# The attention product of an adaLN block: tiles 10 to 15 in pairs, with seven products of half blocks

## The reference

```python
h = _layernorm(x, axis=-1) * (1 + ca) + sa
x = x + ga * _L0_attn_ref(h, mask, weight, bias)      # h @ (masked weight).T + bias, 1024 x 1024
h = _layernorm(x, axis=-1) * (1 + cb) + sb
x = x + gb * _L0_ffn_ref(h, gate_w, gate_s, up_w, up_s, down_w, down_s)   # silu(gate) * up, then down; 2752 wide
```

## Time and profile before

| | us |
|---|---|
| median of 3 runs | 1109.13 (1108.66 to 1110.12) |
| profiled execution | 1108.23 |
| its span, first to last instruction | 1106.2 |
| PE busy in the span | 1080.2 (98%) |
| DVE, ACT, POOL busy | 738.5, 427.8, 378.7 |
| attention products of all 16 tiles | 227.1 us busy as shown |

### The profile page before, as it was taken

The page is one execution under the profiler, slowest core; times in us unless marked ns, Lnnn a source line. Parts: engine busy times, 40 slices in busy tenths (PEclk is TensorE's granted clock), DMA queues, the critical chain, the costliest instruction groups (busy, mean ns, idle before and its releaser), DMA issues. The chain is left out here.

```text
span 1106.2 us, 13336 instructions
## 1 busy us (share of the span) xinstructions
PE 1080.2 (98%) x4753; PEld 501.8 (45%) x4753; DVE 738.5 (67%) x939; ACT 427.8 (39%) x783; POOL 378.7 (34%) x348
## 2 busy tenths in 40 slices
PE   5999999999999999999999999999999999999998
PEld 3444444545544444444444444444444444444444
DVE  4456578776687998889797888879545434334434
ACT  2322156555564554546555555555532000000000
POOL 2116346547643442325455555655200000000000
PEclk9999999999999999999999999999999999999999
DMA  9994313234453555445766666675289666566430
GB/s 343 387 388 118 89 64 95 78 94 162 148 200 129 166 175 164 133 125 163 205 204 177 180 200 180 184 204 178 77 350 335 244 248 241 220 241 239 191 127 38
DMA packets 132049, 206.94 MB, mean 187 GB/s; under 512 B 20624, under 2 KB 99216, under 8 KB 129552
## 3 DMA queue, kind: packets, MB, share of 16 engines
q1 hardware_dynamic: 126688, 184.08, 50.9%
q0 software_dynamic: 5296, 22.02, 5.6%
HBM read 137.39 MB, written 68.68 MB: 186 GB/s over the span
## 5 line engine op out<-in xcount | busy, mean ns | idle before, releaser
L1435 PE MATMUL pA<-work 128*128 128x512 f16 x1680 | 377.1, 379 | 4.4 <-ACT work L1099 2.6
L1435 PEld LDWEIGHTS pA<-work 128*128 128x128 f16 x1680 | 163.5, 98 | 205.1 <-ACT work L1099 6.5
L1238 PE MATMUL pA<-work 128*128 128x512 f32 x512 | 227.1, 595 | 2.5 <-DVE work L1694 0.9
L1435 PE MATMUL pB<-work 128*128 128x512 f16 x752 | 175.9, 379 | 1.4 <-DVE work L1855 1.4
L1238 PEld LDWEIGHTS pA<-work 128*128 128x128 f32 x512 | 94.3, 190 | 113.4 <-issue 110.4
L1877 DVE SCALAR_TENSOR_TENSOR work<-work 128x512 f16<-128x512 f16 x144 | 123.2, 878 | 19.1 <-ACT work L1119 18.8
L1502 PE MATMUL pA<-work 128*128 128x512 f16 x600 | 134.4, 379 | 0.0
L1099 ACT ACTIVATE work<-pA 128x512 f32<-128x512 f32 x126 | 74.6, 592 | 113.3 <-PE pA L1435 108.0
L1435 PEld LDWEIGHTS pB<-work 128*128 128x128 f16 x752 | 73.5, 98 | 90.1 <-DVE work L1855 2.1
L948 ACT ACTIVATE work<-pB,small 128x128 f32<-128x128 f32 x240 | 86.5, 476 | 69.5 <-PE pB L1211 58.1
L1502 PE MATMUL pB<-work 128*128 128x512 f16 x480 | 107.5, 379 | 0.5 <-DMA work<-h_left_scratch 0.5
(11 more groups left out here) (178 smaller groups left out, 1060.5 us busy)
## 6 DMA issues: line engine op xcount, KB each, us to landing
work<-h_scratch SPq DMA_DIRECT2D x8, 4480.0 KB, 13.7
h_scratch<-work SPq DMA_DIRECT2D x60, 512.0 KB, 3.3
work<-in_L_wmod SPq DMA_DIRECT2D x10, 2048.0 KB, 16.1
work<-in_L_ffn_gate_w SPq DMA_DIRECT2D x84, 128.0 KB, 3.3
work<-in_L_ffn_up_w SPq DMA_DIRECT2D x84, 128.0 KB, 3.0
work<-down_scratch SPq DMA_DIRECT2D x7, 1280.0 KB, 11.5
work<-in_L_ffn_down_w SPq DMA_DIRECT2D x68, 128.0 KB, 2.8
work<-in_L_attn_data SPq DMA_DIRECT2D x16, 512.0 KB, 4.3
```

What stands on the lines that cost most here:

```text
L1238: last = pe.matmul(pA[:, 2 * par(t) + h, :], hT1[par(t)][:, c, :], wT[:, c, h * H:(h + 1) * H], start=(c == 0), stop=(c == KT - 1))
L1435: last = pe.matmul(ps, w[:, m, c], bc[b][:, mv_, s, c], start=begin, stop=(i == n - 1 and c == KT // 2 - 1 and s == 1), skip_group_check=True)
```

## The change

Tiles 0 to 9 stay as they are. Tiles 10 to 15 are taken in three pairs (a, b). For a pair, the product of the two tiles (2 x 128 rows) by the weight (1024 x 1024) is seen as a 2 x 2 by 2 x 2 block product: a_11, a_12 are the two halves of the inner dimension of tile a, a_21, a_22 those of tile b, and w_11 to w_22 are quarters of the weight. Seven products of half blocks, with sums and differences of the a and w blocks, take the place of eight. In detail:

- POOL makes the weight combinations t_1, t_2, t_4 at tiles 3, 4 and 5 (`weight_combos`, two additions of 128 x 1024 each) and one more in place in the first pair; for each pair it makes four combinations of the turned inputs in place in `hT1` (128 x 512 each).
- PE runs the products 1, 2, 5, 6, 3, 4, 7 of four matmuls each, with four banks that change roles from pair to pair. One bank holds a running sum.
- ACT copies the running sum to `x1` three times a pair (four copies of 128 x 512), and turns tiles out in halves.
- DVE adds the other banks to these copies (five additions a pair), then multiplies by `ga` in SBUF.
- The weight combinations lie where rows 6 and 7 had their place (`bc0[3]`), so rows 6 and 7 now pass through `stage` and DRAM too, and are loaded back after the sixth product of the last pair; group 0 of the gate and up products waits for that load.
- The orders of all engines from tile 10 on are new.

The core of the diff:

```diff
-    bc_d = nc.dram_tensor("combos_scratch", (2, P, HE), F16).ap()
+    bc_d = nc.dram_tensor("combos_scratch", (3, P, HE), F16).ap()
...
+        F0 = 10
+        PAIRS = [(t, t + 1) for t in range(F0, NT, 2)]
+        NP = len(PAIRS)
+        PRODUCTS = [1, 2, 5, 6, 3, 4, 7]
...
-            for u in range(EARLY, EARLY + 2):
-                load_unit(u)
-
-            sp.wait_ge(attn_done, NT)
+            load_unit(EARLY)
+            sp.wait_ge(stage_stored, 16)
+            sp.wait_ge(attn_done, multiplied(NP - 1, 6))
+            sp.dma_start(bc0[NJ - 1].rearrange("p m s e -> p (m s e)"), bc_d[0]).then_inc(bc0_loaded, 16)
+            sp.wait_ge(attn_done, ATT_END)
...
+                if t in (3, 4, 5):
+                    weight_combos(t - 3)
+            rstd_of(0, F0 + 1)
+
+            for i, (a, b) in enumerate(PAIRS):
+                if i == 0:
+                    sums(b - 4)
+                pool.wait_ge(hT1_ready, b + 1)
+                pool.tensor_tensor(s_1, a_21, a_22, ALU.add).then_inc(combos_made, 1)
+                pool.wait_ge(combos_made, made(i, 1))
+                pool.tensor_tensor(a_21, a_11, a_21, ALU.subtract).then_inc(combos_made, 1)
+                pool.wait_ge(combos_made, made(i, 3))
+                pool.wait_ge(attn_done, multiplied(i, 1))
+                pool.tensor_tensor(a_11, s_1, a_11, ALU.subtract).then_inc(combos_made, 1)
+                rstd_of(1, b - 2)
+                pool.wait_ge(combos_made, made(i, 2))
+                pool.wait_ge(attn_done, multiplied(i, 2))
+                pool.tensor_tensor(a_12, a_12, a_11, ALU.subtract).then_inc(combos_made, 1)
+                if i == 0:
+                    for k in range(2):
+                        c = slice(2 * k, 2 * k + 2)
+                        pool.tensor_tensor(w_12[:, c], w_22[:, c], w_12[:, c], ALU.subtract).then_inc(combos_made, 1)
+                if b < LAST:
+                    rstd_of(0, a + 2)
+                after_residual(b - 2)
...
+                pool.dma_start(bc_d[i], stage.rearrange("p m s e -> p (m s e)")).then_inc(stage_stored, 16)
+                if b < LAST:
+                    rstd_of(0, b + 2)
+                if i:
+                    pair_sums(i - 1)
+                sums(b - 2)
+                rstd_of(1, a)
+                after_residual(a)
...
+            for i, (a, b) in enumerate(PAIRS):
+                if i == 0:
+                    act.wait_ge(attn_done, F0)
+                    turn_out_of_pair(b, 1)
+                else:
+                    act.wait_ge(attn_done, multiplied(i - 1, 7))
+                turn_out_of_pair(b, 0).then_inc(hT1_ready, 1)
+                hi_part(b - 4)
+                copy_product(i, 1, 1, a, (0,))
+                second_input(a - 2)
...
+                copy_product(i, 3, 7, b, (1, 0))
+            cast_unit(4)
+            cast_unit(5)
...
+            for i, (a, b) in enumerate(PAIRS):
+                R, X, Z, Y = pair_banks(i)
...
+                pair_product(R, a_11, two_halves(w_11), True)
+                transpose(1, a - 2)
...
+                pair_product(X, a_12, two_halves(w_21), True)
...
+                pair_product(Z, s_1, two_halves(t_1), True)
...
+                pair_product(R, a_11, two_halves(t_2), False)
+                if b < LAST:
+                    transpose(0, a + 2)
+                transpose(1, b - 2)
...
+                pair_product(X, a_12, two_halves(w_22), True)
+                pair_product(Y, a_22, t_4, True)
+                if b < LAST:
+                    transpose(0, b + 2)
...
+                pair_product(R, a_21, two_halves(w_12), False)
+            transpose(1, LAST - 1)
...
                 if g == 0:
-                    pe.wait_ge(pair_free, LAST - 2)
+                    pe.wait_ge(bc0_loaded, 16)
+                    pe.wait_ge(pair_free, freed(NP - 1, 2))
...
+            for i, (a, b) in enumerate(PAIRS):
...
+                lo_part(b - 4)
+                dve.wait_ge(attn_done, multiplied(i, 2))
+                plus(i, 1, x1a[0], X).then_inc(pair_free, 1)
+                normalise(1, b - 2)
+                if i < 2:
+                    turn_unit(2 * i + 1)
+                if b < LAST:
+                    norm1(a + 2)
+                    norm1(b + 2)
+                dve.wait_ge(attn_done, multiplied(i, 3))
+                link(plus(i, 2, x1a[1], X))
+                plus(i, 2, x1a[1], Z).then_inc(pair_free, 1)
+                gated(a, freed(i, 2))
+                if i < 2:
+                    turn_unit(2 * i + 2)
+                lo_part(a - 2)
+                normalise(1, a)
+                dve.wait_ge(attn_done, multiplied(i, 7))
+                plus(i, 3, x1b[1], Z).then_inc(pair_free, 1)
+                dve.tensor_tensor(x1b[0], x1b[0], Y, ALU.subtract).then_inc(pair_free, 1)
+                gated(b, freed(i, 4))
+            turn_unit(5)
```

More of the change, by code:

```diff
@@ L305, in adaln_kernel @@
         bma_copied = sem("bma_copied")
-        m_loaded = [sem(f"m_loaded{k}") for k in range(8)]
+        m_loaded = [sem(f"m_loaded{k}") for k in range(6)]
         w_loaded = [sem(f"w_loaded{k}") for k in range(8)]
@@ L491, in par, with multiplied, made, freed @@
             return t % 2
+        F0 = 10
+        PAIRS = [(t, t + 1) for t in range(F0, NT, 2)]
+        NP = len(PAIRS)
+        PRODUCTS = [1, 2, 5, 6, 3, 4, 7]
+        ATT_END = F0 + 7 * NP
+        def multiplied(i, product):
+            return F0 + 7 * i + PRODUCTS.index(product) + 1
+        def made(i, what):
+            return 6 + 4 * i + (2 if i else 0) + (1, 3, 2, 4)[what - 1]
+        T3_MADE = 12
+        def freed(i, k):
+            return F0 - 2 + 4 * i + k
+        def copied(i, k):
+            return 2 + 3 * i + k
+        def pair_banks(i):
+            return [bank[k] for k in ((0, 1, 2, 3), (1, 2, 0, 3), (2, 0, 1, 3))[i % 3]]
         def place(t):
@@ L518, in combos_of @@
             j = t // 2
-            return bc0[j] if j < NJ else bc1[j - NJ] if j - NJ >= 2 else stage
+            return bc0[j] if j < NJ - 1 else bc1[j - NJ] if j - NJ >= 2 else stage
         def stored_pair(q):
@@ L1038, in cast_unit @@
                         act.wait_ge(p3_done, last_group_of(c - NWC) + 1)
+                    if c == 2 and g == 0:
+                        act.wait_ge(attn_done, multiplied(NP - 1, 4))
                     dst = wc[c % NWC][:, (A11, S3)[g]:(A11, S3)[g] + 2]
@@ L1063, in _ @@
             evacuate(1)
-            for t in range(2, NT + 1):
-                if 11 <= t <= LAST and t != 13:
-                    hi_part(t - 3)
-                if t <= LAST - 1:
-                    turn_out(t + 1)
+            for t in range(2, F0):
+                turn_out(t + 1)
                 if t == 2:
@@ L1830, in _ @@
             residual(5)
-            for t in range(6, NT + 1):
-                if t <= LAST - 2:
-                    stats1(t + 2)
+            for t in range(6, F0):
+                stats1(t + 2)
                 if t in (6, 7, 8):
                     lo_part(2 * t - 12)
-                if t == 10:
-                    lo_part(6)
-                    lo_part(7)
-                if 11 <= t <= LAST:
-                    lo_part(t - 3)
-                if t <= LAST - 2:
-                    normalise(0, t + 2)
-                if t in MID and t > 4 and t <= LAST:
-                    normalise(1, MID[t] + 1)
-                if t <= LAST:
-                    residual(t)
+                normalise(0, t + 2)
+                normalise(1, MID[t] + 1)
+                residual(t)
                 if t in END:
```

168 lines of the change are left out of this document (122 added, 46 removed).

## The result

The changed kernel takes 1149.6 us (median of four runs, 1148.96 to 1151.92) against 1109.0 of the kernel before on the same chip: a ratio of 1.0368, 95% interval 1.035 to 1.0386. It is slower by 3.7%; the prediction was 1145.0 in a range of 1116 to 1160. The profiled execution took 1149.08 us, span 1147.3, against 1108.23 and 1106.2: 41.1 us of span to be explained.

The account below looks back on a forecast made before the run. PE alone bounds the old kernel there; in the changed one a ring through DVE and POOL sets each pair. 1108.2 + 29.5 (pairs) + 3.6 (weight combinations) + 3.7 (end of stage) = 1145.0 us, range 1116 to 1160.

Parts of the forecast that it names:

- Weight combinations: Six POOL additions of 2.36 us at tiles 3 to 5, delaying row 2's transposes: 3.6 us counted, ends 0 and 6.5.
- The stage: Three pairs, tiles 10 to 15: 39.0, 39.9 and 42.9 us plus 0.9 make 122.7 where 93.2 stood: +29.5.
- idle time of 13 to 16 us per pair: Sign: PE idle this long in each pair, ahead of the transposes, released by DVE's normalisations.
- a rival of its own: PE at its lower clock after the waits: 5 to 20 us more, 1150 to 1165; chance 0.08.
- the ring: Chain through DVE and POOL in each pair: 39.9 us, against 27.5 that PE needs and 31.0 now.
- End of the stage: ACT's cast of unit 5 stands before group 0's first snapshot and waits for DVE: PE waits 3.7 us.
- the 15 us of groups behind it hide nothing: Step: the feed-forward groups after the snapshot wait absorb none of it, as PE is the bound there too.
- Rows 6 and 7 through DRAM: Load lands 10.2 us after issue, PE has 12.1 us ahead: costs nothing, 0 to 2 if slow.
- the five stops: DVE's standstills per pair: 0.9, 2.4, 4.1, 2.1 and 4.6 us, for roots, bias additions, load of x and sums; together 14.1.
- the turns on the port: DVE and POOL instructions exclude each other on the SBUF port; besides the five stops, 2.3 us counted per pair.
- the bound of 1120: If port turns cost nothing: pairs of 34.3, 33.7 and 33.0 us, +12 with 3.7 at the end.
- The rival of a faster kernel: The ring closes within PE's work if the five stops shrink from 14.1 to 4 us: 1098 or 1102; chance 0.08.

Follow-up runs that it names:

- e1: Changed kernel with 14 to 32 small PE products of 128x128, results never read, ahead of six of the waiting transposes; 1147.55 us, ratio 1.0351.
- e9: Changed kernel with ACT's cast of down unit 5 moved behind the snapshot, alone; 1149.31 us, ratio 1.0347.
- e3: Changed kernel with POOL's bias addition and store of tile b-2 moved ahead of the fourth combination; 1144.89 us, ratio 1.032.
- e4: Changed kernel with POOL's root of row a ahead of its pair's last sum, DVE's normalisation of it ahead of the low part; 1146.68 us, ratio 1.034.
- e6: Changed kernel with e3, e4, e9, weight combinations at tiles 3, 3, 4, and tile a+2's statistics and first normalisation at the pair's start; 1132.05 us, ratio 1.0206.
- e7b: Changed kernel with each two-input POOL addition in its loop, from the first pair on, replaced by two write-only fills; 1135.66 us, ratio 1.0236.
- e8: Changed kernel with five of each pair's seven products over half their contraction, 25.8 us of PE products left out; 1146.86 us, ratio 1.0341.

## Why the prediction was right, step by step

In the profiles the 41.1 us of span come as follows; behind each the prediction's own term.

- *The start, 1.4 us, forecast 0.* The transposes at 65.45 us start at 66.84. An edit that the list of the change doesn't name does this, as shown below the list.
- *Weight combinations, 5.5 us, forecast 3.6 with ends 0 and 6.5.* Mechanism and place were right: row 2's transposes waited 3.75, and 1.63 of the kernel before were taken up. The mis-sized term is what follows a wait: eight transposes at 1.97 in place of 1.04 and sixteen records at 8.90 in place of 7.03, 2.8 us; a small wait of 0.6 before it was not forecast either. The recorded 3.6 is also 0.3 short of its own working, 5.5 less 1.63.
- *The stage, 29.7 us (216.60 to 340.34 against 209.72 to 303.79), forecast 29.5.* The pairs took 41.6, 38.2 and 42.2 us from first product to first product (the second eight of the 16 records at 256.55 and 294.72), by the prediction 39.0, 39.9 and 42.9. The waits came where they were written down: tile 12, row 10, tile 14, row 12, row 14, and the first sum. Only row 13's did not come: its transposes at 320.08 ran on. The sizes were less good: tile 12 6.7 us for 8.4 forecast, row 10 2.7 for 5.7, tile 14 4.1 for 6.7, row 12 4.9 for 7.3, row 14 7.2 for 4.7. The sign "idle time of 13 to 16 us per pair" failed: it was 9.2, 6.9 and 12.1, and the waits that the prediction itself lists give 10.4, 12.4 and 16.3. So the agreement of the sum hides an exchange and is in part luck. The prediction wanted 39.1 us of waits (its pair of 39.0 holds another 1.1 that it doesn't name); measured are 28.1 us of waits and 11.2 us of longer records. It gave the lower clock to a rival of its own, as something on top of the ring. The clock did fall, and it came out of the waits: what PE loses to it, it waits less for DVE. e1 shows that, with 0.6 us in the stage for the 11.2.
- *End of the stage, 2.3 us, forecast 3.7.* The wait is the cast's, as forecast, and e9 removes it; it was 1.91, and 16 products at 4.36 (3.62 in e1) add 0.7, of which 0.4 come back before the down products. That removing it would gain its length was not borne out: in e9's profile the later wait took it, and the timed runs show no gain.
- *Down products, 2.3 us, forecast none.* PE waits 2.8 us for `h_left_scratch` where it waited 0.5; the chain of that load is a store of 12.9 us and a load of 15.6, where the load took 13.5; why it takes longer stays open. In the other runs the wait lies between 1.2 and 3.5 and follows no edit. The prediction's step "the 15 us of groups behind it hide nothing" stopped short of this wait.
- *Rows 6 and 7 through DRAM, 0.* No wait of PE for that load stands in the view of waits; the page gives 10.6 us from issue to landing (10.2 in the earlier trace rows).

The start, in DVE's rows of the kernel before and of the changed kernel:

```profile
41.68 2.58 DVE L1700 TENSOR_REDUCE work<-work 128x32 f32<-128x1024 int32 x2 [7.80 <-DMA work<-in_L_attn_mask]
```

```profile
43.30 2.34 DVE L1867 TENSOR_REDUCE work<-work 128x32 f32<-128x1024 int32 x2 [9.05 <-DMA work<-in_L_attn_mask]
```

These are the two reductions of the third quarter of the mask. The loads that they read landed at 41.66 and 43.01 us before and at 41.24 and 43.28 after. Before, each reduction starts when its own load has landed, at 41.68 and 43.04; now the first starts when both have, at 43.30, and the second behind it at 44.44, 1.4 us later than before, of which the later landing is 0.3. The diff joins the two semaphores:

```diff
-                    dve.wait_ge(m_loaded[2 * q + i], 16)
+                    if q < 2:
+                        dve.wait_ge(m_loaded[2 * q + i], 16)
+                    else:
+                        dve.wait_ge(m_loaded[q + 2], 32)
```

So the tiles 0 to 9 did not stay quite as they were, and the prediction's list of changes, and with it its sum, lacks this place. In all eleven changed kernels the first of these reductions starts within 0.03 us of the second landing; no run puts the old wait back.

Both halves of the sum, the five stops and the turns on the port, were borne out separately: e3, e4 and e6 took stops out by order alone, e7b took the turns out with the stops left. How much of the loss the turns are is known from one side only: the prediction put them at 25 us (1145.0 less the bound of 1120), e7b takes out 13.9, but leaves those of the normalisations in part (1.41), and DVE's waits for the load of x grow from 7.5 to 13.2 us; the fills, on the other hand, are somewhat shorter than the additions. The rival of a faster kernel needed the ring to be shorter than PE's 27.5 us; the pairs took 38 us and more, and e8 shows that PE's work is not why.

## What to carry to other kernels

Before work is taken from the bounding engine, lay out the chain of the others for one period of the new order, with their waits and not only their busy shares: here DVE and POOL had a third of their time free, and the chain through both was still 40 us where PE needed 27.5. Where two engines take turns on a port, as here, an instruction that waits for another engine's result should be able to start before that engine's next long instruction: it took 2.83 us in place of 0.81. Count what a wait is worth where the next wait is: removing 1.9 us gave nothing that could be told, while of the 4.6 us that an order won at the end of the stage 3.9 were left at the end of the profile. And read the whole diff when the orders are compared: one joined semaphore far from the pairs cost, by the rows above, 1.1 us.

## What the runs showed of the hardware that was not expected

- PE's clock falls inside this stage. After waits of 4.94 and 7.16 us eight transposes take 1.97 us against 1.04, after 1.93 us sixteen records of products 8.80 against 7.03; the stretches' granted clocks are 0.87 to 0.91, a mix of the levels of 1.2 and 2.4 GHz. The prediction had no row for this. The Trainium skill, "TensorE: Matmul & The Clock Gate", Part 1, says that idle time lowers it, and these rows agree; that filling the waits with products restores 0.96 to 1.00 (e1) and that this shortens the stage by only 0.6 us is this kernel's own.
- A write-only fill on POOL leaves DVE's two-input additions at 1.22 us (1.89 and 1.45 beside POOL's additions), but still takes turns with the normalisation: 1.41.
- POOL starts its next instruction 0.07 us before the normalisation that its last result released, at 263.36 and at 280.56 against 263.43 and 280.63, so that the port is taken when DVE comes.
